# Row sums of attention from each score tile instead of from pairs, two score banks throughout, and a coarser layer-norm copy

## The reference

```python
B, T, D_MODEL, N_HEADS, HEAD_DIM, H = 2, 4096, 2048, 16, 128, 8192
q = (x @ Wq.T + bq).reshape(B, T, N_HEADS, HEAD_DIM).transpose(0, 2, 1, 3)
k = x @ Wk.T + bk                      # one head of 128
v = x @ Wv.T + bv
scores = einsum('bhtd,bsd->bhts', q, k) / sqrt(HEAD_DIM)
scores = where(pos_s < pos_t, scores, -1e30)
attn = softmax(scores) * row_valid     # row 0 has no valid key
out = einsum('bhts,bsd->bhtd', attn, v).transpose(...).reshape(B, T, D_MODEL) @ Wo.T + bo
x = layernorm(x + out)
hidden = fwht(silu(x @ W1.T) * (x @ W3.T))   # Walsh-Hadamard over 8192, / sqrt(8192)
x = layernorm(x + hidden @ W2.T)
```

## Time and profile before

| | |
|---|---|
| the profiled execution's own time | 2939.83 us |
| its span on the slowest core (core 1) | 2938.1 us |
| spans of the eight cores | 2919.4 to 2938.1 us |
| TensorE matmul busy | 2373.3 us, 81% |
| VectorE busy | 660.2 us, 22% |
| ScalarE busy | 632.7 us, 22% |
| chain that ended last, share of TensorE | 74% |
| same chain, share of the reciprocal (L484) | 4% |

### The profile page before, as it was taken

The page is one execution under the profiler, slowest core; times in us unless marked ns, Lnnn a source line. Parts: engine busy times, 40 slices in busy tenths (PEclk is TensorE's granted clock), DMA queues, the critical chain, the costliest instruction groups (busy, mean ns, idle before and its releaser), DMA issues.

```text
span 2938.1 us, 28624 instructions; the slowest of 8 cores (2919.4 to 2938.1 us)
## 1 busy us (share of the span) xinstructions
PE 2373.3 (81%) x9792; PEld 914.4 (31%) x9792; DVE 660.2 (22%) x1056; ACT 632.7 (22%) x1131; POOL 162.1 (6%) x304
## 2 busy tenths in 40 slices
PE   3889846666677677793999999999999999879793
PEld 1223301111111122232444444444444434334341
DVE  1111255555554544214000000000000000001002
ACT  1221222343455455006111111111111100001001
POOL 1210110000000000000000000000000000000000
PEclk9777955677888888895999999999999999889897
DMA  7853462222000000203222222222222235446453
GB/s 218 262 169 124 144 212 90 86 86 72 1 0 1 1 1 1 86 29 143 65 65 72 72 65 72 65 72 72 65 66 71 72 100 154 137 140 194 141 153 129
DMA packets 96466, 276.73 MB, mean 94 GB/s; under 512 B 11716, under 2 KB 11844, under 8 KB 91976
## 3 DMA queue, kind: packets, MB, share of 16 engines
q0 software_dynamic: 37968, 156.26, 17.2%
q1 hardware_dynamic: 58360, 118.65, 12.8%
HBM read 224.54 MB, written 50.33 MB: 94 GB/s over the span
## 4 chain that ended last, share of the span: by engine, by line
PE 74%; DVE 10%; DMA 6%; issue 5%; ACT 5%; DVEq 0%; ACTq 0%; POOL 0%; SPq 0%; POOLq 0%
PE pb L177 71%; DVE GA L484 4%; PE pb L179 2%; DVE pb L443 2%; DMA GA<-X1S 2%; DMA GA<-XBT 2%; ACT GA L690 1%; DVE GA L416 1%; ACT GA L240 1%; DMA W2P<-GA 1%; DVE GA L244 1%; DMA GA<-W2P 1%; ACT GA L571 1%; ACT GA L446 1%; DVE GA L750 0%
## 5 line engine op out<-in xcount | busy, mean ns | idle before, releaser
L177 PE MATMUL pb<-GA 128*128 128x512 bf16 x8576 | 2070.2, 397 | 173.1 <-DVE GA L750 47.4
L177 PEld LDWEIGHTS pb<-GA 128*128 128x128 bf16 x8576 | 824.0, 100 | 1329.8 <-issue 506.1
L446 ACT ACTIVATE GA<-pb 128x512 bf16<-128x512 f32 x576 | 323.9, 596 | 409.8 <-PE pb L177 291.3
L177 PE MATMUL pb<-GA,CB 128*1 128x512 bf16 (+1 forms) x416 | 165.0, 421 | 186.2 <-DVE GA L416 181.1
L670 DVE TENSOR_TENSOR GA<-GA,pb 128x512 bf16<-128x512 f32 x128 | 82.3, 684 | 903.2 <-ACT GA L667 883.8
L690 ACT ACTIVATE GA<-pb 128x512 bf16<-128x512 f32 x128 | 69.6, 595 | 840.8 <-PE pb L177 840.8
L179 PE MATMUL pb<-GA,CB 64*64 64x512 bf16 x512 | 116.8, 483 | 77.2 <-ACT GA L240 50.3
L416 DVE TENSOR_TENSOR GA<-GA 128x512 bf16<-128x512 bf16 x288 | 119.5, 422 | 209.2 <-PE pb L177 118.9
L244 DVE CAST GA<-pb 128x512 bf16<-128x512 f32 x128 | 83.1, 687 | 306.3 <-PE pb L179 304.7
L177 PEld LDWEIGHTS pb<-GA,CB 128*1 128x1 bf16 (+1 forms) x416 | 35.3, 85 | 360.2 <-issue 345.3
L750 DVE TENSOR_TENSOR GA<-pb,GA 128x512 f32<-128x512 f32 x32 | 20.6, 686 | 495.4 <-PE pb L177 436.0
(11 more groups left out here) (49 smaller groups left out, 411.8 us busy)
## 6 DMA issues: line engine op xcount, KB each, us to landing
GA<-W2P SPq DMA_DIRECT2D x256, 256.0 KB, 2.6
GA<-W2T POOLq DMA_DIRECT2D x128, 256.0 KB, 4.8
W2P<-GA SPq DMA_DIRECT2D x128, 256.0 KB, 5.1
GA<-W1S POOLq DMA_DIRECT2D x64, 512.0 KB, 3.9
GA<-W3S POOLq DMA_DIRECT2D x64, 512.0 KB, 3.8
GA<-XBT POOLq DMA_DIRECT2D x8, 2048.0 KB, 13.8
GA<-WQS POOLq DMA_DIRECT2D x4, 2048.0 KB, 10.6
GA<-XOWN SPq DMA_DIRECT2D x1, 8192.0 KB, 34.1
```

Of the source, the lines that this page charges most:

```text
L177: return e.matmul(out, lhsT, rhs, start=start, stop=stop, skip_group_check=True)
L446: texp = em.op("s", lambda e, qp=qp, slot=slot: e.activation(pbuf[slot], qp[:], AF.Exp, scale=SC), waits=_mx(dep, pbuf_rd[slot]))
```

## The change

1. In the K/V stage the four transposes of a block go into the four quarters of one bank (4 or 5 in turn), and one copy of 128x512 takes the place of four of 128x128.
2. In the attention VectorE's additions of pairs are gone; each tile has its own row-sum matmul, straight behind its value matmul and with no wait of its own. `pbuf` has 8 slots in rotation instead of 6 and two for the sums. The number of row-sum matmuls goes from 288 to 576.
3. The score matmuls use banks 0 and 1 throughout. Before, they used 0, 1, 6 and 7 once `p0_step` was through, which is from k = 4.
4. In the first layer norm the conversion to bfloat16 is one ScalarE instruction of 128x2048; before, ScalarE did one half and VectorE the other. `x1tm` lies where the attention output was (`O_C`), the place that the W1 buffers take next, and so the first loads of W1 and W3 wait for the end of the layer norm; before, they waited for the output projection.

```diff
@@ key and value blocks
-            for st in range(4):
-                sig = blk * 4 + st
-                bank = 4 + st % 2
-                pt = pb[bank]
-                mmt = em.op("t", lambda e, pt=pt, sl=sl, st=st: MM(
-                    e, pt[:, 0:128], vTs[sl][:, st * 128:st * 128 + 128], IDN,
...
-                tevt = em.op("s", lambda e, pt=pt, sig=sig: e.copy(
-                    vP[:, sig * 128:sig * 128 + 128], pt[:, 0:128]),
-                    waits=_mx(mmt))
...
+            bank = 4 + blk % 2
+            pt = pb[bank]
+            for st in range(4):
+                mmt = em.op("t", lambda e, pt=pt, sl=sl, st=st: MM(
+                    e, pt[:, st * 128:st * 128 + 128],
+                    vTs[sl][:, st * 128:st * 128 + 128], IDN,
...
+            tevt = em.op("s", lambda e, pt=pt, blk=blk: e.copy(
+                vP[:, blk * 512:blk * 512 + 512], pt[:]),
+                waits=_mx(mmt))
@@ attention
-                if p0_state["i"] >= 64 and len(QKB) == 2:
-                    QKB = (0, 1, 6, 7)
...
-                    if len(rsp) == 2:
-                        (sa, ta_, fa, la_), (sb, tb_, fb, lb_) = rsp
...
-                        va = em.op("v", lambda e, sa=sa, sb=sb, psl=psl: e.tensor_add(
-                            pbuf[psl], pbuf[sa], pbuf[sb]),
-                            waits=_mx(ta_, tb_, pbuf6_rd[psl - 6]))
-                        rs = em.op("t", lambda e, psl=psl, fa=fa, lb_=lb_: MM(
-                            e, pb[4][0:1, :], ONEC, pbuf[psl], fa, lb_),
-                            waits=_mx(va, rs_rd, tCB) if fa else _mx(va))
...
+                    rs = em.op("t", lambda e, slot=slot, first=first,
+                               last_av=last_av: MM(
+                        e, pb[4][0:1, :], ONEC, pbuf[slot], first, last_av),
+                        waits=_mx(rs_rd, tCB) if first else ())
+                    pbuf_rd[slot] = rs
...
-                        bank = QKB[qctr % len(QKB)]
-                        qctr += 1
-                        slot = sig_ctr % 6
+                        bank = QKB[sig_ctr % 2]
+                        slot = sig_ctr % 8
@@ first layer norm
-        x1tm = [vb(O_KSQ + i * 4096, 2048) for i in range(2)]
+        x1tm = [vb(O_C + i * 4096, 2048) for i in range(2)]
...
-            ct0 = em.op("s", lambda e, k=k: e.copy(
-                x1tm[k % 2][:, 0:1024], S1[k % 2][:, 0:1024]),
-                waits=_mx(nm, x1tm_rd[k % 2]))
-            ct1 = em.op("v", lambda e, k=k: e.tensor_copy(
-                x1tm[k % 2][:, 1024:2048], S1[k % 2][:, 1024:2048]),
-                waits=_mx(nm, x1tm_rd[k % 2]))
+            ct = em.op("s", lambda e, k=k: e.copy(x1tm[k % 2], S1[k % 2]),
+                       waits=_mx(nm, x1tm_rd[k % 2]))
@@ feed-forward
-        w1_rd = [_mx(wo_rd[0], wo_rd[1]), _mx(wo_rd[0], wo_rd[1])]
-        w3_rd = [_mx(wo_rd[0], wo_rd[1]), _mx(wo_rd[0], wo_rd[1])]
+        w1_rd = [_mx(tX1T, x1tm_rd[0], x1tm_rd[1]), _mx(tX1T, x1tm_rd[0], x1tm_rd[1])]
+        w3_rd = [_mx(tX1T), _mx(tX1T)]
```

More of the change, by code:

```diff
@@ L306, in build_program @@
             ps_tok[2 + sl] = tev
+            bank = 4 + blk % 2
+            pt = pb[bank]
+            mmt = None
             for st in range(4):
-                sig = blk * 4 + st
-                bank = 4 + st % 2
-                pt = pb[bank]
                 mmt = em.op("t", lambda e, pt=pt, sl=sl, st=st: MM(
-                    e, pt[:, 0:128], vTs[sl][:, st * 128:st * 128 + 128], IDN,
+                    e, pt[:, st * 128:st * 128 + 128],
+                    vTs[sl][:, st * 128:st * 128 + 128], IDN,
                     True, True),
-                    waits=_mx(tev, tCB, ps_tok[bank]))
-                tevt = em.op("s", lambda e, pt=pt, sig=sig: e.copy(
-                    vP[:, sig * 128:sig * 128 + 128], pt[:, 0:128]),
-                    waits=_mx(mmt))
-                ps_tok[bank] = tevt
-                vP_wr.append(tevt)
-                if st == 3:
-                    vT_rd[sl] = mmt
+                    waits=_mx(tev, tCB, ps_tok[bank]) if st == 0 else (),
+                    inc=(st == 3))
+            vT_rd[sl] = mmt
+            tevt = em.op("s", lambda e, pt=pt, blk=blk: e.copy(
+                vP[:, blk * 512:blk * 512 + 512], pt[:]),
+                waits=_mx(mmt))
+            ps_tok[bank] = tevt
+            vP_wr.append(tevt)
             last_kv_mm = mmv
@@ L377, in build_program @@
         recB_rd = [None, None]
-        pbuf_rd = [None] * 6
+        pbuf_rd = [None] * 8
         attnT_wr = []
@@ L381, in build_program @@
         first_attnT = True
-        st3 = {"rb_rd": rb_rd, "rb2_rd": rb2_rd, "fin": None, "pc": 0}
-        pbuf6_rd = [None, None]
-        qctr = 0
+        st3 = {"rb_rd": rb_rd, "rb2_rd": rb2_rd, "fin": None}
         for k in range(J):
             for g in range(NG):
-                if p0_state["i"] >= 64 and len(QKB) == 2:
-                    QKB = (0, 1, 6, 7)
-                    qk_rd[6] = ps_tok[6]
-                    qk_rd[7] = ps_tok[7]
-                    qctr = 0
                 avbank = 2 + (g % 2)
@@ L396, in build_program @@
                 pend = []
-                rsp = []
                 niter = (k + 1) * 4
@@ L408, in emit_avrs @@
                         inc=False)
-                    rsp.append((slot, texp, first, last_av))
-                    rs = None
-                    if len(rsp) == 2:
-                        (sa, ta_, fa, la_), (sb, tb_, fb, lb_) = rsp
-                        del rsp[:]
-                        psl = 6 + (st3["pc"] % 2)
-                        st3["pc"] += 1
-                        va = em.op("v", lambda e, sa=sa, sb=sb, psl=psl: e.tensor_add(
-                            pbuf[psl], pbuf[sa], pbuf[sb]),
-                            waits=_mx(ta_, tb_, pbuf6_rd[psl - 6]))
-                        rs = em.op("t", lambda e, psl=psl, fa=fa, lb_=lb_: MM(
-                            e, pb[4][0:1, :], ONEC, pbuf[psl], fa, lb_),
-                            waits=_mx(va, rs_rd, tCB) if fa else _mx(va))
-                        pbuf6_rd[psl - 6] = rs
-                        pbuf_rd[sa] = _mx(rs, va)
-                        pbuf_rd[sb] = _mx(rs, va)
+                    rs = em.op("t", lambda e, slot=slot, first=first,
[3 more added lines that the diff above has]
+                    pbuf_rd[slot] = rs
                     return rs
@@ L453, in build_program @@
                         if len(pend) == 2:
-                            rs_mm = emit_avrs(*pend.pop(0)) or rs_mm
+                            rs_mm = emit_avrs(*pend.pop(0))
                         pend.append((slot, sig, it == 0, it == niter - 1, texp))
@@ L595, in build_program @@
                         True, True),
-                        waits=_mx(ct0 if c4 < 2 else ct1,
-                                  x1ps_rd[bank], tCB) if ci == 0 else (),
+                        waits=_mx(ct, x1ps_rd[bank], tCB) if ci == 0 else (),
                         inc=(ci == 3))
```

6 lines of the change are left out of this document (2 added, 4 removed).

## The result

The changed kernel takes 2875.34 us (median of 11 runs, lowest 2869.20); the kernel before has a median of 2939.96 over 33 runs, lowest 2921.18. The ratio is 0.9796, with a 95% interval of 0.9776 to 0.9815, about 60 us less. The forecast was 2884, 56 us less. (The ratio leaves out executions in which the cores of one die ran at a lower clock; those account for the highest times.) The profiled execution of the changed kernel took 2872.85 us, its slowest core 2871.3.

The account below looks back on a forecast made before the run. It took attention as the place to gain, TensorE idling 181.1 us before row-sum matmuls for VectorE's pair sums. Attention -63, K/V -6, layer norm +8.4, W1 load +4.3 make -56 on 2939.83: 2884 us, range 2860 to 2908.

Parts of the forecast that it names:

- The stall behind the reciprocal goes: Attention, change of groups, k of 4 and up: TensorE's wait behind VectorE's reciprocal disappears, giving back 3.85 us a group.
- The price of a row-sum matmul: Attention: 0.216 us plus 0.19 for two shape changes, 0.41 at full clock; an undisturbed tile then costs 0.84 us.
- Rival 2: Attention: a row-sum matmul costs only 0.216 us, its shape change hidden; 60 us more saved, 2824 us; chance 0.08.
- A group at full clock: Attention, k of 4 and up: groups take 20.2, 23.6, 26.9 and 30.3 us, saving 50 us before clock falls.
- The clock's falls: Attention, k of 4 and up: remaining half-rate time costs 1.0 us a group, 16 in all, leaving 34 us gained.
- Rival 1: Attention: the clock falls as long as before, so no change, about 2945 us; chance 0.14.
- k = 1 to 3: Attention, earlier groups: 10 us gained at k = 1 and 17 us at k = 2 and 3.
- K/V: K/V stage: four transposes without copies between save 0.9 us a block, six blocks showing, 6 us gained.
- The first W1 load: Start of the feed-forward: the load now starts when TensorE would start and takes 4.3 us to land, 4.3 lost.
- Rival 3: Attention, plain tiles, k of 4 and up: clock stays at 0.50, each tile 1.48 us, 3109 us; chance 0.07.
- rival 4: Attention: the clock goes to 0.81 as in Q, 65 us lost over some 430 plain tiles, 2949 us; chance 0.05.
- rival 5: Attention: the stall stays because something else of `fin` holds TensorE; about +60 us, 3000 us; chance 0.04.

Follow-up runs that it names:

- norec_before: Kernel before the change with each group's reciprocal replaced by a multiplication by a constant; ratio 0.9763 to the kernel before, lowest 2849.02 us.
- spread: Kernel before the change with each group's reciprocal cut into four 128-column instructions, one every second tile of the next group; ratio 0.9706, median 2852.12 us.
- wide_ones: Changed kernel with a stationary operand of 128 columns of ones for the row-sum matmul; ratio 0.9439 to the kernel before, median 2765.52 us.
- filler: Changed kernel with six more matmuls a group, which nobody reads, from k = 4 on; ratio 0.9699 to the kernel before, median 2844.13 us.
- norec_after: Changed kernel with each group's reciprocal replaced by a multiplication by a constant; ratio 0.9683 to the kernel before, median 2837.12 us.

## Why the prediction was right, step by step

- **The stall behind the reciprocal goes** (3.85 us a group). Right: the 5.11 us of the earlier trace rows became 0.63. `norec_before` and `spread` take the stall away or shorten it by other means and gain about the same. That the pair sums go was one way among several to empty VectorE's queue; leaving them out was not the source of the gain in the late groups.
- **The price of a row-sum matmul** (0.41, a tile at 0.84). Right: 0.845. `wide_ones` shows that the change of shape makes it up. Rival 2, which had it free, falls.
- **A group at full clock** (20.2, 23.6, 26.9, 30.3). Right to 0.1: with the clock held at 2.4 GHz `filler` has 20.24, 23.62, 27.00 and 30.38. So the working of the stall, of the diagonal tiles (those with a mask) and of the group's end holds as a sum; the single terms weren't measured one by one.
- **The clock's falls** (1.0 us a group from k = 4 on, 16 in all). This term was too small: the falls cost 25 us, 1.6 a group, and k of 4 and up gave 23.3 us instead of 34. The estimate took less than one fall of 3.4 us a group. On core 5 of the changed kernel the clock records show twelve falls in the sixteen groups, six of 3.4 us and six of 6.8, a mean of 3.85 us at 1.2 GHz a group (9.2 in the kernel before); a group of k = 5 takes 23.8, 25.1 or 26.1 us, by how much of a fall lies in it, against 23.62 without. That is between the forecast and Rival 1, nearer the forecast.
- **k = 1 to 3** (10 + 17 = 27). Too small as well, the other way: 19.8 + 25.5 = 45.3. The granted clock went from 0.52 to 0.75 at k = 1 and from 0.73 to 0.84 at k = 2 and 3, which the working left out: it priced the stall alone. By the clock records a group of k = 1, 2 and 3 has 21.9, 13.5 and 14.9 us at 1.2 GHz in the kernel before and 8.2, 7.5 and 6.0 in the changed one (means over the cores). No run holds the clock there in the changed kernel; `norec_after` shows that these groups follow it.
- **k = 0** (2): 2.7, from 66.1 to 63.4 us between the first reciprocal and the fourth.
- **K/V** (6 gained). The step at one block is right (0.87 a block), the sum is 3.7 to 4.3, less than six times that. How many of the blocks pass it on wasn't counted.
- **The layer norm** (8.4 lost): 7.1. A copy of 2048 columns takes 1.90 and not twice 1.04, 0.86 more a block.
- **The first W1 load** (4.3 lost): 5.4. The direction and the reason are right: the wait is for the DMA.
- **The rest**: 3.4 us less ahead of the first exponential, where the change does nothing. `spread`, which is the kernel before in that stretch, takes 149.5 us there, like the other runs; what the profiles before and after have above that are the cores at 0.81. It is no effect of the change.

So two misses, 11 us short from k = 4 on and 18 over at k = 1 to 3, partly cancel in the total, and that is luck: the attention gave 71 to 73 us instead of 63, and the sum came out nearer than its parts. Rival 1 (falls as long as before) fell with the rise of the clock in every window from k = 4 on (0.89 to 0.94, where 0.81 to 0.86 were). Rival 3 fell with the 1.00 in the plain tiles, rival 4 with the same row, rival 5 with the missing idle time behind the broadcast.

What stays open: why the clock falls less at k = 2 to 4 once the reciprocal is short, and which part of the change gains at k = 1 and 2 what `spread` doesn't. A run that holds the clock there, as `filler` does from k = 4 on, would tell what these groups cost without it.

## What to carry to other kernels

A long instruction (here 3.4 us) on an in-order queue holds up everything short behind it, and the price is paid by the engine that waits for the short ones, and a second time by that engine's clock: cut the long one in pieces, put it later, or take the short ones off its queue. Before adding matmuls of another operand shape into a dense stream, count two changes of shape each; a full-width operand that computes the same was cheaper here, and made a broadcast needless. A stage that gains from removed stalls gains again at the clock, so predict it with the clock of the stage after, not of the stage before.
